# One program per engine for a three-stage vision tower kernel, with the weight preparation between the stages moved into the stages

## The reference, cut to what matters

```python
# 1. mix (S4D kernel): the rows of the sequence
K = 2.0 * einsum('chn,hnl->chl', Cc, exp(dtA[:, :, None] * arange(1024))).real   # (32, 128, 1024)
h = concatenate([cls_tok, K], axis=1)                                            # (32, 129, 1024)
# 2. attention, 32 heads of 32, 8 key/value heads, causal, rotary positions
h = h + attention(layernorm(h), Wq, Wk, Wv, Wo)
# 3. a dense layer with weights and activations rounded to 8 bits
h = h + (fake_quant_per_token(layernorm(h)) @ fake_quant_per_channel(w).T + b)
```

## Time and profile before

| | us |
|---|---|
| median of 3 runs (1679.89 to 1681.06) | 1680.6 |
| the profiled execution | 1692.21 |
| its span, first to last instruction | 1690.4 |
| PE busy in the span | 1576.1 (93%) |
| DVE busy | 1213.1 (72%) |
| ACT busy | 888.1 (53%) |
| POOL busy | 615.0 (36%) |

### The profile page before, as it was taken

How to read it: one execution, slowest core, us unless ns; L and a number is a source line. 1 busy time by engine, 2 the same in 40 slices (tenths; PEclk the granted TensorE clock), 3 DMA queues, 4 the chain that set the end, 5 groups by cost and what they waited for, 6 DMA issues and landing times. The chain is left out here.

```text
span 1690.4 us, 35578 instructions
## 1 busy us (share of the span) xinstructions
PE 1576.1 (93%) x11802; PEld 1254.9 (74%) x11802; DVE 1213.1 (72%) x2262; ACT 888.1 (53%) x2928; POOL 615.0 (36%) x632
## 2 busy tenths in 40 slices
PE   4888889999999999999999999937799999999997
PEld 2788868888888888888888888826577777777774
DVE  8997556676767666676767666537588888888885
ACT  7576427777777777777777777722311111111110
POOL 0322024444444444444444444410133333333333
PEclk8889989999999999999999999958899999999998
DMA  8345501101010101101010100043233233332221
GB/s 211 75 104 121 150 26 39 44 33 50 25 50 31 43 31 43 47 28 50 25 50 31 43 31 20 27 184 125 90 112 101 96 101 112 112 111 100 94 92 44
DMA packets 59160, 122.64 MB, mean 73 GB/s; under 512 B 9345, under 2 KB 29954, under 8 KB 59106
## 3 DMA queue, kind: packets, MB, share of 16 engines
q1 hardware_dynamic: 59106, 121.94, 23.1%
HBM read 71.18 MB, written 51.66 MB: 73 GB/s over the span
## 5 line engine op out<-in xcount | busy, mean ns | idle before, releaser
L764 POOL TENSOR_TENSOR pool_a<-pool_a,ri 128x512 f32<-128x512 f32 x256 | 266.4, 1041 | 459.4 <-DVE ri L1126 459.4
L984 ACT ACTIVATE pool_a<-sm,ml 128x128 f32<-128x128 f32 x1024 | 399.4, 396 | 19.7 <-DVE ml L1119 18.7
L836 PE MATMUL att_ps<-w_lo,xT_hi 128*128 128x512 f32 x768 | 325.9, 424 | 0.0
L836 PE MATMUL att_ps<-w_hi,xT_lo 128*128 128x512 f32 x768 | 304.2, 396 | 0.0
L836 PE MATMUL att_ps<-w_hi,xT_hi 128*128 128x512 f32 x768 | 304.1, 396 | 0.0
L1110 DVE TENSOR_TENSOR sm<-att_ps,cst 128x512 f32<-128x512 f32 x256 | 173.3, 677 | 142.6 <-PE att_ps L884 142.6
L997 ACT COPY pool_a<-att_ps 128x512 f32<-128x512 f32 x256 | 149.5, 584 | 164.0 <-PE att_ps L893 164.0
L1435 PE MATMUL ffn_ps<-wo_hi,cT_hi 128*128 128x512 f32 x528 | 215.6, 408 | 3.0 <-DVE cT_lo L1578 3.0
L1435 PE MATMUL ffn_ps<-wo_hi,cT_lo 128*128 128x512 f32 x528 | 206.8, 392 | 0.0
L1435 PE MATMUL ffn_ps<-wo_lo,cT_hi 128*128 128x512 f32 x528 | 206.0, 390 | 0.0
L984 ACT ACTIVATION_READ_ACCUMULATOR pool_a<-sm,ml 128x1 f32 x1024 | 196.6, 192 | 0.0
(11 more groups left out here) (213 smaller groups left out, 2510.5 us busy)
## 6 DMA issues: line engine op xcount, KB each, us to landing
h_in<-h_rows SPq DMA_DIRECT2D x33, 512.0 KB, 4.3
h_rows<-pool_b SPq DMA_DIRECT2D x64, 256.0 KB, 3.7
hbuf<-h_rows SPq DMA_DIRECT2D x32, 512.0 KB, 3.7
ctx_turned<-pool_a SPq DMA_DIRECT2D x64, 256.0 KB, 2.0
ctx_in<-ctx_turned SPq DMA_DIRECT2D x32, 512.0 KB, 3.6
out_dram<-pool_b SPq DMA_DIRECT2D x32, 512.0 KB, 2.8
pool_a<-in_L_attn_Wq_dram SPq DMA_DIRECT2D x8, 512.0 KB, 18.2
pool_b<-in_L_attn_Wo_dram SPq DMA_DIRECT2D x2, 2048.0 KB, 13.4
```

The costliest lines, as they stand in the source:

```text
L764: G.tensor_tensor(pr[:, g % 4], pr[:, g % 4], ri[:, g % 2, :].unsqueeze(2).to_broadcast([P, GQ, P]), ALU.mult).then_inc(p_ready, 1)
L836: mm = nc.tensor.matmul(bank[:], lhs, w_part[:, e, blk * BK:(blk + 1) * BK], start=(r == 0), stop=(r == EC * 3 - 1))
L984: a = nc.scalar.activation(pr[:, g % 4, q, :], sm[:, g % 2, q, :], ACT.Exp, bias=ml[:, b[1], 0, h:h + 1], accum_out=ml[:, b[1], 1, h:h + 1])
```

## The change

All three stages are written as functions that return five engine programs, and one block runs, per engine, the mix part, the attention part and the last part. Where a buffer is reused by the next stage, a semaphore of the stage before is waited for. SBUF and PSUM are laid out by hand at fixed addresses for that. In the parts:

- **Mix.** From step 1 on the phases are computed by POOL (`phase`), not by DVE. DVE's order is now: coefficients of half 0, powers, whole turns of k+1, coefficients of half 1, all of step k. The real half of the tables is turned while DVE works on the imaginary half. The first 8 of the 24 rounds for Wk and Wv are put between the last four units of step 7 (`between`), in the PSUM banks that the tables held.
- **Attention.** The tail tile is projected first, alone, as iteration -1; the last 8 rounds of Wq are spread over it. `nth(tile)` is the place in this new order. The rounding and turning of `w` is spread over iterations -1 to 3: DVE `round_w` (8 units), POOL `quantise_w`, PE `turn_w`, ACT `store_w`. Wo is loaded in iteration 31, and its 16 rounds lie two by two in the 8 steps of iteration 32. Iteration 33 holds the 48 matmuls of the output projection of tile 0, six per step.
- **Last stage.** It starts with tile 1. What `merge_last_rows` did is cut into three pieces on DVE, behind tiles 1, 2 and 3.

```diff
@@ mix: DVE
-            coefficients(0, 0)
-            turns_of(1)
-            coefficients(0, 1)
-            for k in range(NCP):
-                if k + 2 < NCP:
-                    turns_of(k + 2)
-                if k + 1 < NCP:
-                    powers(k + 1)
-                    coefficients(k + 1, 0)
-                    coefficients(k + 1, 1)
+        coefficients(0, 0)
+        whole(1)
+        coefficients(0, 1)
+        for k in range(1, NCP):
+            coefficients(k, 0)
+            powers(k)
+            if k + 1 < NCP:
+                whole(k + 1)
+            coefficients(k, 1)
@@ mix: POOL
-            for k in range(1, NCP):
-                pool.wait_ge(wholes, k + 1)
-                at_least(pool, powers_ready, k)
-                nc.gpsimd.tensor_tensor(yb[:, k % 2], yb[:, k % 2], kb[:], ALU.subtract).then_inc(fracs, 1)
+        def phase(k):
+            at_least(pool, sin_done, k - 1)
+            for h in range(CP):
+                t = nc.gpsimd.tensor_scalar(yb[:, k % 2, h, :], iota, rates[:, 1, k * CP + h:k * CP + h + 1],
+                                            quarter, ALU.mult, ALU.add)
+            t.then_inc(phases, 1)
...
+        pool.wait_ge(powers_ready, 1)
+        phase(1)
+        for k in range(1, NCP):
+            fraction(k)
+            if k + 1 < NCP:
+                phase(k + 1)
@@ mix: ACT, in the loop over units i of half `half` of step k
-                        if half == 0 and k + 2 < NCP:
-                            magnitudes(k + 2, 4 * i, 4)
-                    if half == 0 and k + 2 < NCP:
-                        sine(k + 2)
+                    if (k, half) == (NCP - 1, 1):
+                        between(i)
+                    if i < 2 and k + 2 < NCP:
+                        magnitudes(k + 2, 8 * half + 4 * i, 4)
+                    if half == 0 and i == 2 and k + 1 < NCP:
+                        sine(k + 1)
@@ attention: PE, in the 8 steps s of iteration t
+                if at(t, -1) and s < 4:
+                    pe_round(pe, R_CLS + XROUNDS + 2 * s)
+                    pe_round(pe, R_CLS + XROUNDS + 2 * s + 1)
+                u = w_turn_at(t, s)
+                if u is not None:
+                    turn_w(u)
...
+                if at(t, NB):
+                    if s == 0:
+                        pe.wait_ge(rot_ready, NBLK * (NB + 1))
+                    turn_wo(pe, 2 * s)
+                    turn_wo(pe, 2 * s + 1)
+                if at(t, NB + 1):
+                    project_first(pe, s)
@@ attention: iterations
-            body((-1, 1))
+        body((-1, 0))
+        body((-1, 1))
@@ attention: SP
-                sp.wait_ge(projected, NBLK * (NB + 1))
-                load_wo(sp)
-                load_w(sp)
+            if at(t, NB - 1):
+                sp.wait_ge(projected, NBLK * nth(t) + 1)
+                load_wo(sp)
@@ last stage: DVE, behind the work of tile t
+            if at(t, 1):
+                end_scores()
+            if at(t, 2):
+                end_weights()
+            if at(t, 3):
+                end_context()
@@ program: one block
+        with nc.Block() as block:
...
+            @block.tensor
+            def _(pe):
+                mix.tensor(pe, lambda i: turn_first(pe, i))
+                att.tensor(pe, turn_wo, project_first)
+                ffn.tensor(pe)
```

More of the change, by code:

```diff
@@ L40 @@
 GQ = HEADS // HKV
+HALVES = HEADS // 16
 EC = L // P
@@ new lines, in overlaid @@
+def overlaid(nc, ctx, *layouts):
+    tensors = {}
+    for i, layout in enumerate(layouts):
+        with ExitStack() as placed:
+            end = 0
+            for name, first, shape, dtype in layout:
+                assert first >= end and first % 8 == 0, name
+                if first > end:
+                    placed.enter_context(nc.sbuf_tensor(f"gap{i}_{end}", [P, first - end], F32))
+                tensors[name] = placed.enter_context(nc.sbuf_tensor(name, [P] + list(shape), dtype))
+                end = first + -(-columns(shape, dtype) // 8) * 8
+                assert end <= ARENA, name
+    ctx.enter_context(nc.sbuf_tensor("arena", [P, ARENA], F32))
+    return tensors
@@ new lines, in pe_round @@
+    def pe_round(pe, r):
+        kind, i = ROUNDS[r]
+        if r == 0:
+            pe.wait_ge(products, 2 * NCP)
+        if r == R_MIX:
+            pe.wait_ge(rows_out, 8 * NCP)
+        if r >= 4:
+            pe.wait_ge(hi_done, r - 3)
+            pe.wait_ge(lo_done, r - 3)
+        if kind == "x" and i == 0:
+            pe.wait_ge(cls_xn_ready, 1)
+        if kind == "w" and i % EC == 0:
+            pe.wait_ge(raw_in[i // EC], 32 if i == 0 else 64)
+        bank = ps[r % 4 + (4 if r < R_MIX else 0)]
+        for q in range(4):
+            src = xn[:, (4 * i + q) * P:(4 * i + q + 1) * P] if kind == "x" else \
+                raw[i // EC][:, q, (i % EC) * P:(i % EC + 1) * P]
+            mm = nc.tensor.transpose(bank[:, q * P:(q + 1) * P], src, ident)
+        mm.then_inc(turned, 1)
@@ new lines, in ffn_stage, with project @@
+    PARTS = ((cT_hi, wo_hi), (cT_hi, wo_lo), (cT_lo, wo_hi))
+    def project(pe, t, n0, n1):
+        u = number(t)
+        for n in range(n0, n1):
+            half, r = divmod(n, PER_HALF)
+            e, part = divmod(r, 3)
+            if n == 0:
+                pe.wait_ge(c_hi, 2 * u + 2)
+                pe.wait_ge(c_lo, 2 * u + 2)
+            if r == 0:
+                at_least(pe, resid, 2 * u + half - 1)
+            c_part, w_part = PARTS[part]
+            mm = nc.tensor.matmul(O_BANK[half][:], c_part[:, t[1], e, :], w_part[:, e, half * BK:(half + 1) * BK],
+                                  start=(r == 0), stop=(r == PER_HALF - 1))
+            if r == PER_HALF - 1:
+                mm.then_inc(out_proj, 1)
```

2760 lines of the change are left out of this document (1408 added, 1352 removed).

## The result

| | us |
|---|---|
| before, median of 4 | 1680.4 |
| after, median of 4 (1651.3 to 1654.2) | 1653.0 |
| ratio after / before | 0.9836 [0.9819, 0.9853] |
| forecast | 1615.0 (1600 to 1638) |

The change makes the kernel 27.4 us faster; 65.6 were forecast. The profiled execution of after took 1653.0 us too (span 1651.2), so here the profile stands for the timed runs.

What follows compares the result with a forecast made beforehand. PE is 93% busy, so gains lie only where it is not: seams, weight preparation, mix loop. Terms sum to -65.6 us, taken from the timed 1680.6 to give 1615.0; range for 8 in 10: 1600 to 1638.

Steps and rivals of the forecast that it cites:

- I keep the difference: Final time: the timed median is 11.6 us below the profiled execution; keeping that gives 1680.6 - 65.6 = 1615.0.
- Iteration 32: End of attention, with 16 Wo rounds and no tail: ACT's load of 28.1 us bounds it; 28.5 us, +3.2.
- Iteration 33: End of attention: 48 matmuls of tile 0 (11 us) between attention work of 6.5 us; 17.5 us, +4.1.
- Rival B: Lockstep in iteration 32: PE's Wo rounds in two banks wait for DVE's copies, queued behind softmax; +12, 1627, chance 0.13.
- The prediction's own sign: End of attention: the prediction is wrong if iterations 32 and 33 together take over 60 us.
- Last stage: From the end of iteration 33 to the end: 506 us in place of 529.6, -23.6, of which 15.4 is weight preparation.
- PE's wait of about 3 for tile 0: Start of the last stage: tile 0's chain to its transpose takes 8.75 us, PE work covers only 5.5.
- Weight preparation: Iterations 1 to 3: three turns of 8 transposes and three ACT copies, +4; w's turn in iteration -1 within its 1.5-us term.
- Mix loop: First stage: PE bounds the loop, which ends at 166.0 in place of 190.5 us; -24.5 with the start.
- the lock: Mix loop: the exclusive VectorE-GpSimd port pair could hold up powers or phases; 2.07 us a meeting, 14.5 at most.
- The price p = 0.35: Mix loop: estimated us for one phase instruction on POOL; up to 0.52 allowed before POOL's chain exceeds 14.3 a step.
- First seam: Between mix loop and first projection: a chain through cls' load and transposes of 21.5 us in place of 30.5, -9.0.

Runs made afterwards that it cites:

- experiment 1: The kernel before, unchanged, profiled again: ratio 1.0001, profiled execution 1680.7 us, span 1678.9.
- Experiments 2 and 3: Changed kernel, in iteration 32: VectorE's lower parts of Wo one step later, 1643.0 us; instead ScalarE's copies of Wo ahead of the exponentials, 1640.7 us.
- Experiment 4: Changed kernel, with POOL waiting for the bias before its first addition, not before its first power: 1642.1 us, ratio 0.9772.
- kernel 7: Changed kernel without the weight preparation, the last stage working on a constant in place of the weights: ratio 0.9742.
- experiment 9: Changed kernel, with the second rounding step of w on ScalarE instead of POOL: ratio 0.9804.
- experiment 11: Changed kernel, with the first eight rounds of turned weights back in the seam behind the mix loop: 1649.5 us, ratio 0.9815.

## Why the prediction was wrong

It was right in direction and 38.0 us short in size: 27.4 us came, and 65.6 were forecast. By its own steps ("old profile" is the one that the prediction read, "new profile" is that of experiment 1):

| stretch, us | forecast change | measured, old profile | measured, new profile |
|---|---|---|---|
| to the first product | -1.4 | -1.4 | -1.4 |
| mix loop, to its last copy | -23.1 | -24.1 | -15.8 |
| first seam | -9.0 | -7.3 | -7.3 |
| iteration -1 | +24 | +26.3 | +26.3 |
| iterations 0 to 31, to tile 31's transposed queries | +4 | +8.2 | +8.1 |
| from there to the end | -60.1 | -40.9 | -37.6 |
| sum | -65.6 | -39.2 | -27.7 |

*"I keep the difference": 11.6.* This is the step that failed most. The prediction took 24.5 us from a mix loop that was 8.3 longer than in the other profile, and then took the profile's 11.6 off once more. What the change removes cannot also be kept. The row was there: the loop's granted clock of 0.91. The new profile has 0.97 in it. The other 26.4 us are in the stretches that follow. (A slip in the sum goes the other way: the 11, 3 and 3.6 us of tile 1 are 17.6 and not 18.3.)

*Iteration 32: +7.5.* The forecast said that ScalarE's load bounds it, 28.5. What bound it was the circle of waits, 4.86 us a step. Experiments 2 and 3 show it; with the copies ahead the stretch falls by 11.6, and then ScalarE is busy 28.6 of 29.2 us, as the forecast had it. Iteration 33 adds 3.8, since tile 0's lower parts stand at the end of the same queues. Rival B named the lockstep, with +12, and got 0.13. It had the softmax in the way right, but closed the circle through PE's two banks; that its size fits the 11.3 of both iterations is in part luck. The prediction's own sign, over 60 us for the two iterations, did not show: they took 57.3.

*Last stage: +7.8.* No term had the bias. It is issued behind the last context's stores, in SP's order, and the first power of the stage stands behind its arrival on POOL. In the old profile of before the bias was issued at 1148.2, in the seam, and the first power ran at 1175.7. Experiment 4 gives 10.9, with the clock. Two terms were too high and hide some of it: PE's wait of about 3 for tile 0 is 1.2 once the bias is out of the way, and the merge costs 3.4 by the distances of tiles 1 to 4 over 14.93 (5 forecast), 0.9 of them on PE.

*Weight preparation: 4.5 forecast, 15.2 measured.* It shows as only 2.3 + 4.1 in the table, since two other things were better than forecast and hid it: in kernel 7, without the preparation, iteration -1 takes 22.6 us (23.5 by the forecast), and iterations 0 to 31 take 3.2 us less than before. The prediction had traded that start, no longer cold, for four turns of w, at 0. Of the missing price about half is POOL's rounding, 2.77 us a block (6.0 of 12.8 us by experiment 9); the rest is open.

*Mix loop: right, in part by errors that cancel.* Forecast end 166.0, measured 165.0. Over 64 units at PE's own price, the prediction put 1.9 us for the first matmuls at the low clock; the first step is 2.9 over 14.3. It put 2.3 for small misses; they are 1.5, in the last three steps, and they are POOL's, by one phase a step which is held by the powers. It put 4.0 for the rounds; they cost 2.7 (experiment 11). PE bounds the loop, as forecast, until POOL's lag reaches it. The prediction weighed the lock and let VectorE carry it; it was POOL that lost. The price p = 0.35 was low too (0.44 without a meeting, 0.56 in the mean).

*First seam.* -9.0 forecast, -7.3 measured. cls' transposes start 14.35 us behind the last copy (14 by the forecast); from them to the first projection it is 8.9, not 7.5. The rounds in the loop bought nothing (experiment 11).

## What to carry to other kernels

Before taking differences of a profile, compare its execution with the timed runs; if it is longer, look for the stretch where the granted clock is low, take a second profile, and take the excess out of that stretch, once. Before reading a difference of two stretches, look how far the same stretch differs between executions of the same code. When work is merged into a full pipeline, write the chain of one step through all queues: an instruction put behind another that waits closes a circle as long as the sum of its members, though no engine is full. When barriers go, list what each engine's first wait of the next stage stands for; a load that was hidden in the seam is now ordered by what stands before it in its queue.
